# Patch filter of a four-layer image kernel: depthwise taps spread over four engines

## What is computed

```python
def _L1_conv_ref(x, w_in, w_dw, fft_mask, w_out):
    # C = 48, HIDDEN = 144, C2 = 288, P = 8
    y = jnp.einsum('oc,bchw->bohw', w_in, x)
    yp = y.reshape(B, C2, ht, P, wt, P).transpose(0, 1, 2, 4, 3, 5)
    f = jnp.fft.rfft2(yp) * fft_mask[None]
    yp = jnp.fft.irfft2(f, s=(P, P))
    y = yp.transpose(0, 1, 2, 4, 3, 5).reshape(B, C2, H2, W2)
    y = lax.conv_general_dilated(y, w_dw, window_strides=(1, 1), padding=((1, 1), (1, 1)), feature_group_count=C2, ...)
    x1, x2 = jnp.split(y, 2, axis=1)
    g = jax.nn.gelu(x1, approximate=False) * x2
    return jnp.einsum('oc,bchw->bohw', w_out, g)
```

## Time and profile before

| | |
|---|---|
| Median of the runs | 8340.8 us |
| Profiled execution, its own time | 8343.99 us |
| Its span | 8339.0 us |
| Patch filter, from the first fetch of its weights to the start of the next norm | 3518.9 to 4123.2 us |
| TensorE busy over the span | 6705.5 us (80%) |
| VectorE busy over the span | 6983.8 us (84%) |
| ScalarE busy over the span | 5257.7 us (63%) |
| GpSimd busy over the span | 3359.4 us (40%) |

### The profile page before, as it was taken

The page is one execution under the profiler, slowest core; times in us unless marked ns, Lnnn a source line. Parts: engine busy times, 40 slices in busy tenths (PEclk is TensorE's granted clock), DMA queues, the critical chain, the costliest instruction groups (busy, mean ns, idle before and its releaser), DMA issues. The chain is left out here.

```text
span 8339.0 us, 181301 instructions
## 1 busy us (share of the span) xinstructions
PE 6705.5 (80%) x61152; PEld 2911.9 (35%) x61152; DVE 6983.8 (84%) x6264; ACT 5257.7 (63%) x5277; POOL 3359.4 (40%) x1726
## 2 busy tenths in 40 slices
PE   4999999999999999799697788788878878834321
PEld 2533333333333333255332333333333333322110
DVE  7788888888888888788748999999999999964556
ACT  2177777777777777522187888888888888820000
POOL 1000000000000000000007999999999999934666
PEclk9999999999999999899899999999999999967665
DMA  1020000000000000000020000000000000022222
GB/s 27 26 38 5 5 5 5 7 5 5 5 5 5 7 5 5 4 0 0 12 60 15 6 6 6 6 6 6 6 6 6 6 7 6 6 56 74 67 66 74
DMA packets 116941, 139.45 MB, mean 17 GB/s; under 512 B 49884, under 2 KB 96060, under 8 KB 115148
## 3 DMA queue, kind: packets, MB, share of 16 engines
q1 hardware_dynamic: 91488, 76.06, 3.7%
q0 software_dynamic: 24576, 50.36, 2.3%
q10 hardware_dynamic: 256, 3.15, 0.3%
HBM read 93.83 MB, written 35.65 MB: 16 GB/s over the span
## 5 line engine op out<-in xcount | busy, mean ns | idle before, releaser
L1527 POOL TENSOR_TENSOR k_image<-k_image,s_b 128x1024 f32<-128x1024 f32 x1152 | 2697.0, 2354 | 457.9 <-ACT k_image L1437 421.0
L604 ACT ACTIVATE att_prob<-att_scores,a_bound,a_temp 128x1024 f32<-128x1024 f32 x2048 | 2361.4, 1202 | 692.5 <-PE att_scores L542 689.7
L638 DVE TENSOR_TENSOR att_prob_lo<-att_prob 128x1024 f16<-128x1024 f32 x2048 | 2451.1, 1238 | 410.1 <-ACT att_prob L604 365.7
L542 PE MATMUL att_scores<-att_queries,att_keys 64*128 64x512 f16 x12288 | 1520.6, 380 | 22.7 <-DMA att_keys<-qk_halves 19.2
L1437 ACT COPY k_image<-h_du 128x1024 f32<-128x1024 f32 x1152 | 1169.3, 1015 | 434.4 <-PE h_du L1366 433.2
L525 POOL TENSOR_TENSOR k_image<-k_image,att_rden 48x512 f32 x32 | 69.1, 2159 | 3334.2 <-DVE att_rden L653 3334.2
L1487 DVE TENSOR_TENSOR_SCAN h_state_odd<-h_keep,k_image 128x1024 f32<-128x1024 f32 x576 | 1327.1, 2348 | 0.1
L1444 ACT ACTIVATE h_keep<-h_keep,h_decay 128x1024 f32<-128x1024 f32 x1152 | 1258.8, 1093 | 65.2 <-PE h_keep L1354 44.2
L555 PE MATMUL att_sums<-att_prob,a_values 128*64 128x512 bf16 x8192 | 1136.1, 398 | 42.8 <-issue 42.8
L1354 PE MATMUL h_keep<-h_rows,h_spread 128*128 128x512 bf16 x2304 | 703.0, 387 | 466.2 <-DVE k_image L1487 217.9
L542 PEld LDWEIGHTS att_scores<-att_queries,att_keys 64*128 64x128 f16 x12288 | 540.6, 94 | 928.8 <-issue 627.0
(11 more groups left out here) (275 smaller groups left out, 7293.3 us busy)
## 6 DMA issues: line engine op xcount, KB each, us to landing
y_rows<-h_y_sb SPq DMA_DIRECT2D x1024, 3.0 KB
att_queries<-qk_halves SPq DMA_DIRECT2D x256, 48.0 KB, 2.0
parts<-t_part SPq DMA_DIRECT2D x48, 192.0 KB, 2.5
h_rows<-parts SPq DMA_DIRECT2D x128, 72.0 KB
b_shared<-cells,b_index POOLq DMA_INDIRECT x512
att_keys<-qk_halves SPq DMA_DIRECT2D x64, 96.0 KB, 7.2
cells<-b_shared SPq DMA_DIRECT2D x4, 1536.0 KB, 5.1
qk_halves<-qkv_hi SPq DMA_DIRECT2D x32, 112.0 KB, 1.8
```

What stands on the lines that cost most here:

```text
L542: last = nc.tensor.matmul(scores[:, u % 2, r * BLK:(r + 1) * BLK], keys[part, j, g * KT:(g + 1) * KT], queries[part, slot, j, :], start=j ...
L604: nc.scalar.activation(prob[:, j, :], scores[:, j % 2, :], ACT.Exp, bias=bound[:, 0:1], scale=temp[:, 0:1]).then_inc(prob_ready, 1)
L638: nc.vector.tensor_tensor(prob_lo[:, j, :], prob[:, j, :], prob_hi[:, j, :], ALU.subtract).then_inc(low_ready, 1)
L1527: nc.gpsimd.tensor_tensor(drive[k % 3], du_sb[k % 3], b[:, c * CH:(c + 1) * CH], ALU.mult).then_inc(drive_ready, 1)
```

## The change

It is confined to the patch filter, apart from two hooks in `group_norm`.

- Group a: TensorE does the 9 diagonal matmuls only for the upper four rows of a patch row. The lower four rows are 9 taps of 128 x 512 on VectorE (`tap_high`).
- Group b stays on VectorE (`tap_gate`, 9 of 128 x 1024).
- Group c: the slab now holds the upper four rows in partitions 0 to 47 and the lower four in 64 to 111. ScalarE multiplies by each tap's weights (`scale_c`, 9 of 112 x 512), GpSimd adds the nine (`sums`, 8 of 112 x 512) and does c's gate (one more). The inverse transform writes c with 8 matmuls of 64 columns in place of 4 of 128; ScalarE copies the rows across the two halves (`join`, `halos`).
- `stage` and the copy of `x_t` go from VectorE to ScalarE.
- The mix has three PSUM banks instead of two; the transposes use spare columns of the third. The inverse of group a starts with each mask product by itself.
- `output` and `gate` of row `r - 2` both lie in iteration `r`, and the order on each engine is new.
- The weights are fetched and the tiles cleared beside the group norm; mask and diagonals are made there by GpSimd.

```diff
+        if beside_sync is not None:
+            block.sync(beside_sync)
+        if beside_pool is not None:
+            block.gpsimd(beside_pool)
...
+        group_norm(nc, "gn1", image, gmean, norm, sems, False, beside_sync=load_weights, beside_pool=prepare)
...
+            def depthwise(k, ph, t0, t1):
+                if t0 == 0:
+                    pe.wait_ge(placed, k * PLACES + 4)
+                    pe.wait_ge(halo, k * HALOS + 1)
+                    wait_past(pe, gelu_a, 2 * k - 1)
+                for t in range(t0, t1):
+                    src = slab_a[:, ph, t // 3:t // 3 + HALF, t % 3:t % 3 + W]
...
+            def output(k, hh, ncol=BLK):
+                pe.wait_ge(gated_a, k + 1)
+                wait_past(pe, added, k * 2 + hh)
+                nc.tensor.matmul(ps_o[:, 0:ncol], w_oa[:, :], gate_a[:, hh, 0:ncol], start=True, stop=False)
+                pe.wait_ge(gated_c, k + 1)
...
+                if hf == 0 and conv:
+                    depthwise(r - 1, 1 - ph, 0, EARLY_TAPS)
+                if hf == 1 and out:
+                    output(r - 2, 1)
...
+                if hf == 0 and out:
+                    output(r - 2, 0)
+                if conv:
+                    depthwise(r - 1, 1 - ph, *((EARLY_TAPS, MIDDLE_TAPS), (MIDDLE_TAPS, TAPS))[hf])
...
+                    wait_past(pe, masked, q * 4 + max(0, t - Y_BANKS + 1))
+                    nc.tensor.matmul(ps_y[:, t % Y_BANKS, 0:MIX], spec[:, t, :], w_in[:, :], start=True,
...
+                for part, y0 in ((upper, 0), (lower, HALF)):
+                    for t in range(4):
...
+            def scale_c(k, ph, taps, nrow=HALF):
+                act.wait_ge(halo, k * HALOS + (4 if nrow == HALF else 3))
+                for t in taps:
+                    wait_past(act, sum_c, (k - 1) * ADDS + max(t, 1))
...
+                    nc.scalar.activation(dst, src, ACT.Copy, scale=dwc[:, t:t + 1]).then_inc(scaled_c, 1)
...
+            def transform(r, hf, ph, conv=True, follow=True):
+                q = r * 2 + hf
+                act.wait_ge(turned, q + 1)
+                wait_past(act, spectrum, q)
+                nc.scalar.copy(x_t[:, :, :], ps_t).then_inc(turned_copied, 1)
+                if follow:
+                    stage(r + (hf + 1) // 2, 1 - hf)
+                if conv:
+                    scale_c(r - 1, 1 - ph, (range(4), range(5, 8))[hf])
                 act.wait_ge(spectrum, q + 1)
                 wait_past(act, mixed, q * 4)
                 nc.scalar.copy(spec[LO, :, :], ps_x[:, :, :]).then_inc(spectrum_copied, 1)
...
+                if hf == 1:
+                    join(r, ph)
+                    if conv:
                         gelus_c(r - 1)
...
+            def before_first_mix(r, ph, out=True):
+
+                for t in range(3):
+                    tap_high(r - 1, 1 - ph, t)
+                if out:
+                    gate(r - 2)
+                tap_high(r - 1, 1 - ph, 3)
+                tap_gate(r - 1, 1 - ph, 0)
+                tap_high(r - 1, 1 - ph, 4)
+                tap_gate(r - 1, 1 - ph, 1)
+                if out:
+                    add(r - 2, 0)
+
+            def before_second_mix(r, ph, out=True):
+
+                for t in range(5, TAPS):
+                    tap_gate(r - 1, 1 - ph, t - 3)
+                    tap_high(r - 1, 1 - ph, t)
+                if out:
+                    add(r - 2, 1)
 
             def iteration(r, ph, out=True):
+                before_first_mix(r, ph, out)
+                mix(r, 0)
+                before_second_mix(r, ph, out)
+                mix(r, 1)
+                for t in range(6, TAPS):
+                    tap_gate(r - 1, 1 - ph, t)
...
+            def sums(k, ncol=BLK):
+
+                for t in range(1, TAPS):
+                    pool.wait_ge(scaled_c, k * TAPS + t + 1)
...
+                    nc.gpsimd.tensor_tensor(acc_c[:, 0:ncol], first, scaled[:, t, 0:ncol], ALU.add).then_inc(sum_c, 1)
+
+            def gate(k, uses, ncol=BLK):
+                pool.wait_ge(gelu_c, 2 * k + uses)
+                nc.gpsimd.tensor_tensor(gate_c[0:SPAN, 0:ncol], gate_c[0:SPAN, 0:ncol], acc_c[:, 0:ncol],
+                                        ALU.mult).then_inc(gated_c, 1)
```

More of the change, by code:

```diff
@@ L683 @@
 PATCH = 8
+HALF = PATCH // 2
 HID = 3 * C
@@ L689 @@
 WP = W + 2
+TAPS = 9
+ADDS = TAPS - 1
+EARLY_TAPS, MIDDLE_TAPS = 3, 5
+PLACES = 6
+HALOS = 4
+Y_BANKS = 3
+TURN_AT = MIX
 def patch_filter_layer(nc, image, gmean, norm, sems, ident, d):
-    group_norm(nc, "gn1", image, gmean, norm, sems, False)
     with ExitStack() as ctx:
@@ new lines, in join, with gelus_a @@
+            def join(r, ph):
+                act.wait_ge(placed, r * PLACES + PLACES)
+                nc.scalar.copy(slab_c[lower, ph, 0:2, :], slab_c[upper, ph, HALF:HALF + 2, :]).then_inc(halo, 1)
+            def gelus_a(k):
+                act.wait_ge(conv_a, k + 1)
+                wait_past(act, product, k * 2 - 1)
+                nc.scalar.activation(gate_a[:, 0, :], ps_d[:, :], ACT.Gelu).then_inc(gelu_a, 1)
+                act.wait_ge(tap_a, k * TAPS + TAPS)
+                wait_past(act, product, k * 2)
+                nc.scalar.activation(gate_a[:, 1, :], acc_a[:, :, :].rearrange("c r w -> c (r w)"),
+                                     ACT.Gelu).then_inc(gelu_a, 1)
@@ new lines, in transform @@
+                if hf == 0:
+                    convolved(r - 2)
+                place(r, hf, ph, 0)
+                if hf == 0:
+                    wait_past(act, tap_b, (r - 1) * TAPS)
+                place(r, hf, ph, 1)
+                place(r, hf, ph, 2)
+                if hf == 1:
+                    join(r, ph)
+                    if conv:
+                        gelus_c(r - 1)
+            act.sem_inc(halo, 3)
+            stage(0, 0)
+            for hf in range(2):
+                transform(0, hf, 0, conv=False)
@@ L908, in _ @@
+            for hf in range(2):
+                transform(1, hf, 1)
+            with act.Fori(1, NPR // 2 - 1) as i:
+                for ph in range(2):
+                    for hf in range(2):
+                        transform(i * 2 + ph, hf, ph)
+            for r in (NPR - 2, NPR - 1):
+                for hf in range(2):
+                    transform(r, hf, r % 2, follow=2 * r + hf + 1 < 2 * NPR)
+            scale_c(NPR - 1, 1, range(TAPS))
             halos(NPR, 0)
-            for hh in range(2):
-                gelus_a(NPR - 1, hh)
+            gelus_a(NPR - 1)
@@ L1000, in _ @@
                     iteration(i * 2 + ph, ph)
[L1001 to L1005 removed]
+            before_first_mix(NPR, 0)
+            before_second_mix(NPR, 0)
+            for t in range(6, TAPS):
+                tap_gate(NPR - 1, 1, t)
+            gate(NPR - 1)
             for hh in range(2):
                 add(NPR - 1, hh)
[L1009 to L1010 removed]
+            dve.wait_ge(halo, NPR * HALOS + 3)
```

393 lines of the change are left out of this document (182 added, 211 removed).

## The result

The changed kernel takes 8362.9 us in the median (8345.8 to 8369.5), 1.0026 of the time of the kernel before, 95% interval [1.0016, 1.0037]: slower by 0.26%, where 8255 us was forecast. The profiled execution took 8365.85 us, its span 8364.0 us. A windows view of it, by the stages that follow one another; the columns are those of the earlier trace rows. Left out are the attention ahead of the first row and the last layer behind the last.

A forecast was written before the change was run, and what follows sets the result against it. TensorE bounds the patch row now, VectorE plus lost turns after. Loop 63, first iteration 2, prologue 15.8 and end 5.6, less 0.5, save 86 us: profiled 8344.0 becomes 8258, median forecast 8255 us; own range 8225 to 8280, overall 8180 to 8300.

The forecast's parts named there:

- rival 4: Patch row: VectorE loses 2.17 us for each of nine GpSimd operations, period 42.2 us, total 8449 us; chance 0.03.
- Period: Patch loop: one patch row falls from 34.4 to 30.2 us, bounds 29 and 32.
- VectorE's own 22.7: Patch row: VectorE's work alone, 12.7 us in the first half and 10.0 in the second.
- The turns: Patch row: each GpSimd operation meeting a tap or gate costs VectorE 1.07 us; five meet in first half, two in second.
- ScalarE's scaling: Patch row: nine scalings for group c, at most 0.60 us each; ScalarE's total of 17 us stays under the period.
- Rival 3, the clock: Patch row: TensorE's gaps of some 3 us put one inverse at half clock, 3 us x 15 = 45, 8300 us; chance 0.05.
- Rival 1: Patch row: GpSimd and VectorE take no turns, as beside the scans; period 26.0 us, total 8189 us; chance 0.17.
- Rivals 2 and 4: Rival 2, patch row: nine GpSimd operations meet at 1.26 us each, period 34.0, 8310 us; with seven 31.5, 8275; chance 0.13.
- Prologue: Ahead of the patch loop: weight fetch and GpSimd's preparation hide beside the 25 us norm with 9 us of cover; -15.8 us.
- the slower first half: First two halves of the patch filter: staging 0.05 slower on ScalarE, longer inverse, shorter mix; +0.5 us.
- The loop: Patch loop: 15 x (34.4 - 30.2) = 63 us saved, and 2 us less in the first iteration.
- The end: After the patch loop: outputs, adds and last image row fall from 55.7 to 50 us; -5.6.

The follow-up runs named there:

- after_filled: Three dummy 128 x 512 matmuls per patch row in TensorE's gap before the fourth mix matmul, scan loop start at 103, against the changed kernel; 0.9913 of the kernel before.

## Why the prediction was wrong, step by step

**The step that failed** is the first sentence: "the layers follow one another with an image-wide norm between them, so only the patch filter matters". They do follow one another, but they share TensorE's code. The unchanged layers were counted at nothing without a look at what their own starts wait for; rows of 3.2 to 3.7 us "<-issue", one for each turn of the scan loop, stand in the trace of before, 29 of them, and say that each turn waits for something that no engine's work explains. The list of waits of the kernel before has them in one line (us in total, times, longest):

```profile
PE h_du L1366 <- issue: 98.6, 29, 3.7
```

Nothing in that trace gives the price of another place, but 98.6 us of such waits, in a layer whose code the edit moves, was a reason to widen the range upwards. As it stood, a slower kernel had a chance of 0.03, and all of it was given to rival 4, hand-overs inside the patch filter; no rival looked outside it. The sum with what was measured: -80 in the patch filter, +99 in the scans, +6 from the rest make +25 us, 8341 + 22 by the medians.

**The patch row was sized nearly right, by terms that were not.** One row of after, by windows and by group:

```profile
3787.90:3818.50 30.60, 26.06 (x131) 16.21 (x130) 28.18 (x30) 15.88 (x29) 14.07 (x9) 0.94 0.00 0
...
L1017 DVE SCALAR_TENSOR_TENSOR p_acc_b<-p_slab_b,p_dwb,p_acc_b 128x1024 f32<-128x1024 f32 x8 | 11.2, 1405 | 0.1
L1123 POOL TENSOR_TENSOR p_acc_c<-p_acc_c,p_scaled 112x512 f32<-112x512 f32 x7 | 10.4, 1487 | 10.7 <-ACT p_scaled L943 9.8
L1017 DVE SCALAR_TENSOR_TENSOR p_acc_a<-p_slab_a,p_dwa,p_acc_a 128x512 f32<-128x512 f32 x8 | 9.9, 1238 | 0.1
L943 ACT ACTIVATE p_scaled<-p_slab_c,p_dwc 112x512 f32<-112x512 f32 x9 | 6.0, 714 | 0.1
L1054 DVE TENSOR_TENSOR p_ym<-p_ps_y,p_mask 128x304 f32<-128x304 f32 x9 | 4.0, 471 | 2.2 <-PE p_ps_y L837 2.0
L1015 DVE TENSOR_SCALAR p_acc_b<-p_slab_b,p_dwb 128x1024 f32<-128x1024 f32 x1 | 1.8, 1756 | 0.0
```

- Period: 30.6 us against 30.2 (34.45 before). VectorE's own 22.7 was right: 30.6 less the two terms that follow is 22.6. The turns: 8 x (1405 - 1278) + 8 x (1238 - 746) + 1756 - 745 ns = 6.0 us, six of 1.0 where seven of 1.07 were forecast (five in the first half as forecast, one in the second where two were). The rest is 2.0 us of waiting for the mix, which the forecast had at nothing. That the period still came out within 0.4 us is luck: the turns were 1.5 too dear and the wait 2.0 too cheap. (The forecast's own sum has a slip as well: 12.7 + 5 x 1.07 is 18.05 and not 17.9, which makes 30.2 of the 30.1, the number that was taken.)
- What is held off isn't told by the number of inputs: the first tap of b, a TENSOR_SCALAR of one tile and a column of weights, was stretched from 745 to 1756 ns.
- ScalarE's scaling takes 714 ns, not at most 600; its 15.88 us stay under the period, so this cost nothing.
- **Rival 3, the clock, came true and was free.** The timeline of the two inverses of a row:

```profile
3787.29 0.78 PE L837 MATMUL p_ps_y<-p_w_in,p_spec 112*128 112x304 f32 x2 [3.09 <-DVE p_ym L1054]
3787.91 3.23 PE L845 MATMUL p_ps_i<-p_inv,p_ym 128*128 128x128 f32 x16
...
3800.98 2.11 PE L845 MATMUL p_ps_i<-p_inv,p_ym 128*128 128x128 f32 x16
```

Behind a gap of 3.09 us the inverse takes 3.23 us in place of 2.11, at 1.2 GHz for most of it, and the row's mean clock is 0.94. The rival's price was 3 us a row; the clock cost TensorE 1.5 with group c's part, and by after_filled the row 0.
- **Rival 1 rested on a misread row.** The prediction says that the scans of the earlier trace rows have two inputs in SBUF. They have one: `keep`, which the scan reads as its first input (h_keep), is `n.ps("keep", ...)` in the kernel, a tile in PSUM. So these rows are no case against the turns, and they don't speak against the rule of the Trainium skill that the prediction cites beside them. What ran beside GpSimd without being stretched in this case is the scans (2348 ns), the mask products (471 ns after, 470 before) and the adds to the image (684 ns in both), all with one input in PSUM; in one stretch of 350 us of the changed kernel's loop, the 34 mask products and 11 adds that overlapped an add of GpSimd lasted 475 and 685 ns at most. The taps, the gate and the attention's product, which were held off, have every tile in SBUF. No run moves a tile from one to the other, so this stays a reading of rows. Without turns the period is 25.0 us, and it needs GpSimd gone.
- Rivals 2 and 4 gave 34.0 us a row with nine full meetings, 31.5 with seven, and 42; no row of after reached any of them, and 17 operations gave 33.9.

**Prologue: right.** GpSimd and SP beside the norm, in the timeline:

```profile
3498.83 0.42 SPq L759 DMA_DIRECT2D p_w_oc<-in_w_out  x1
...
3502.31 5.22 POOL L775 TENSOR_SCALAR p_diag<-k_ident,p_dwa 128x128 f32<-128x128 f32 x9
...
3515.58 0.81 ACT L891 ACTIVATE p_staged_x<-k_image,k_norm 48x512 f32<-48x512 f32 x1 [1.72 <-PEq L94]
```

The fetches are issued 7.5 us after the norm's start, GpSimd is done 16 us after it, and the norm ends at 3515: 7.5 us of cover, 9 were forecast. From the norm's start to the first mask product 30.2 us against 45.7: -15.5, forecast -15.3 with the slower first half.

**The loop**, first to last mask product: 526.4 to 463.9 us, -62.5 where 65 were forecast (63 and the first iteration's 2).

**The end: -2.1 in place of -5.6.** From the last mask product to the next norm 54.2 us, 56.3 before. The last image row, GpSimd and VectorE:

```profile
4032.88 4.03 POOL L1123 TENSOR_TENSOR p_acc_c<-p_acc_c,p_scaled 112x128 f32<-112x128 f32 x7
4037.34 0.45 POOL L1127 TENSOR_TENSOR p_gate_c<-p_gate_c,p_acc_c 112x128 f32<-112x128 f32 x1 [0.42 <-ACT p_gate_c L949]
```

GpSimd's chain starts only when ScalarE has scaled (4031.5), after TensorE's and VectorE's other work, each add starts 0.58 us after the one before it where 0.45 was the estimate, and gelu, gate, product and add follow: 11.1 us from 4028.5 to the norm at 4039.7, where 10 had been reckoned. Most of the rest lies in the two outputs ahead of it, where VectorE waits 3.7 us each for the product: 8.8 us from the gate's end at 4019.6, where 7 had been reckoned.

## A better version

With 8 or 20 instructions of padding ahead of the scan loop, and nothing else, the change does what was forecast: 0.9906 [0.989, 0.9923] and 0.9908 [0.9892, 0.9925] on one chip, 0.9906 [0.989, 0.9923] on another, that is 71 to 82 us less than the kernel before on the same chip (the forecast, 8255 of 8341, is 0.9897). No other kernel that ran and leaves nothing out of the work was faster by more than the spread of its runs.

## What to carry to other kernels

Before an edit ahead of a long loop is priced, look at the first instruction of each of the loop's passes in the trace of before: an idle time that ends with "issue", once for every pass, was here the sign that the place of the code has a price, and where it stands the range should hold one. When a change comes out tens of us off, set the stages of both traces side by side before anything else: the loss may stand in a stage that nobody edited. And where two engines take turns, idle time of the one is where the other's work is free; filling a gap there gives back in lost turns what it gains.

## What was not expected of the hardware

- A turn of the scan loop, with its 2131 TensorE instructions, makes TensorE's first matmul wait 3.4 us in the mean at the cheap places of its start within 256 instructions and 6.6 at 47; the extra fetch per pass was there at 7, 31, 47 and 49 and not at 55, 57, 64, 67 and 151. Its price rose from 1.1 to 3.4 us.
- Behind a gap of 3.1 us in TensorE's work the granted clock was 0.5 for about 3 us of each row of the changed kernel; behind gaps of 0.4 and 1.2 us in after_filled it stayed at 1.00.
- GpSimd's adds stretched VectorE's taps, whose tiles are all in SBUF, and not its mask products and adds to the image, which read PSUM (471 and 684 ns, as before).
- What follows the scans took 1015 to 1028 us on some chips and 900 to 910 on others, in both kernels, so that only runs of one chip can be set side by side.
